# Experts that scale their rows and scatter-add them into one DRAM row per token; a last stage that reads one row and is spread over three engines

## The reference, cut to what matters

```python
x = _layernorm(x + attention(x))
probs = softmax(flat @ gate_W)                       # 4096 tokens x 8 experts
topk_w, topk_idx = top_k(probs, 2); topk_w = topk_w / topk_w.sum(-1)
combine = (one_hot(topk_idx, 8) * topk_w[..., None]).sum(axis=1)
out = 0.5 * gelu(flat @ shared_W + shared_b)
for e in range(8):
    h = gelu(flat @ W1[e] + b1[e])                   # 256 -> 1024
    out = out + combine[:, e:e + 1] * (h @ W2[e] + b2[e])
out = (out - mean) * rsqrt(var + 1e-5) * gamma + beta
x = _layernorm(x + out)
```

## Time and profile before

| | us |
|---|---|
| median of 3 runs | 2104.87 (2103.75 to 2106.13) |
| the profiled execution | 2106.24, of it 2104.6 in the span |
| mean granted TensorE clock | 0.945 |
| DVE busy over the span | 1370.2 |
| PE busy over the span | 1835.4 |
| POOL busy over the span | 212.1 |

### The profile page before, as it was taken

The page is one execution under the profiler, slowest core; times in us unless marked ns, Lnnn a source line. Parts: engine busy times, 40 slices in busy tenths (PEclk is TensorE's granted clock), DMA queues, the critical chain, the costliest instruction groups (busy, mean ns, idle before and its releaser), DMA issues. The chain is left out here.

```text
span 2104.6 us, 31804 instructions
## 1 busy us (share of the span) xinstructions
PE 1835.4 (87%) x10807; PEld 1169.0 (56%) x10808; DVE 1370.2 (65%) x1767; ACT 935.0 (44%) x1362; POOL 212.1 (10%) x295
## 2 busy tenths in 40 slices
PE   2999999999999999999999996998439999999600
PEld 1544454444444445444444442877239999999600
DVE  3577677777767777776776775333766555555388
ACT  3555544455444555445554552122225555555220
POOL 0000000000000000000000000000054444444200
PEclk9999999999999999999999997999669999999855
DMA  7000000000000000000000003442022222222241
GB/s 254 11 21 26 16 21 26 17 20 26 21 16 26 21 16 26 21 21 21 21 26 16 21 16 134 144 156 70 21 79 85 85 85 82 85 82 85 63 154 60
DMA packets 63836, 115.21 MB, mean 55 GB/s; under 512 B 5120, under 2 KB 36224, under 8 KB 61440
## 3 DMA queue, kind: packets, MB, share of 16 engines
q1 hardware_dynamic: 55744, 90.88, 12.7%
q0 software_dynamic: 8000, 23.08, 3.5%
HBM read 79.60 MB, written 34.34 MB: 54 GB/s over the span
## 5 line engine op out<-in xcount | busy, mean ns | idle before, releaser
L418 ACT ACTIVATE a_e<-banks 128x1024 f32<-128x1024 f32 x512 | 496.2, 1022 | 213.4 <-PE banks L334 213.2
L478 DVE TENSOR_TENSOR a_esum<-a_esum,a_e 128x1024 f32<-128x1024 f32 x384 | 469.5, 1223 | 57.5 <-ACT a_e L418 36.3
L348 PE MATMUL banks<-a_e,a_v 128*64 128x512 f32 x2048 | 495.7, 605 | 0.0
L348 PEld LDWEIGHTS banks<-a_e,a_v 128*64 128x64 f32 x2048 | 124.1, 136 | 238.9 <-issue 176.2
L334 PE MATMUL banks<-a_qh,a_kh 64*128 64x512 f32 x1024 | 229.4, 445 | 2.0 <-DVE a_ql L466 1.6
L482 DVE RECIPROCAL a_inv<-banks 128x512 f32<-128x512 f32 x64 | 214.9, 3358 | 15.9 <-PE banks L357 15.9
L475 DVE TENSOR_TENSOR a_esum<-a_e 128x1024 f32<-128x1024 f32 x64 | 78.4, 1225 | 201.9 <-ACT a_e L418 201.9
L334 PE MATMUL banks<-a_ql,a_kh 64*128 64x512 f32 x1024 | 201.5, 390 | 0.0
L334 PE MATMUL banks<-a_qh,a_kl 64*128 64x512 f32 x1024 | 200.8, 389 | 0.0
L1357 ACT ACTIVATE e_g<-banks,e_b1c 128x256 f32<-128x256 f32 x280 | 113.9, 469 | 139.1 <-PE banks L1297 137.8
L334 PEld LDWEIGHTS banks<-a_qh,a_kh 64*128 64x128 f32 x1024 | 95.7, 183 | 139.6 <-issue 123.5
(11 more groups left out here) (206 smaller groups left out, 2733.1 us busy)
## 6 DMA issues: line engine op xcount, KB each, us to landing
attn_out<-a_ot SPq DMA_DIRECT2D x64, 256.0 KB, 2.0
t_ot<-attn_out SPq DMA_DIRECT2D x8, 2048.0 KB, 8.2
a_w<-w_qkv SPq DMA_DIRECT2D x32, 256.0 KB, 3.1
e_w<-w_up SPq DMA_DIRECT2D x8, 1024.0 KB
e_w<-w_down SPq DMA_DIRECT2D x8, 1024.0 KB
o_y<-expert_rows SPq DMA_DIRECT2D x8, 1024.0 KB, 7.8
b_xr<-x_rows SPq DMA_DIRECT2D x4, 1024.0 KB, 12.7
raw<-x_t SPq DMA_DIRECT2D x8, 512.0 KB, 10.5
```

The lines of the kernel that those rows point to most:

```text
L348: mm = pe.matmul(o_acc[slot % 2][h * DH:(h + 1) * DH, :], v[quad % 2][:, n, head], e[n % NE][:, h * BANK:(h + 1) * BANK], start=n == 0, st ...
L418: act.activation(e[n % NE], ring[n % 2], ACT.Exp, scale=SCALE).then_inc(e_ok, 1)
L478: dve.tensor_tensor(acc[:, :], acc[:, :], e[n % NE], ALU.add).then_inc(add_ok, 1)
```

## The change

**Routing.** The two weights, times 2, go into one tile `w_all`, with two more columns of zeros for padding slots. PE turns it, ACT copies it out of PSUM, and SP stores it as `w_rows` in DRAM (66 x 128). SP also copies `shared` (4 MB) to the new DRAM tensor `acc_rows`, one row per token. `places` holds for each slot two numbers: where its weight is in `w_rows`, and which row of `acc_rows` it goes to.

**Experts.** In each chunk POOL gathers the weights of the 256 slots (two more indirect transfers with 4 bytes for each partition) and scatters with an addition in the transfer. ACT scales the bias by the weight; DVE scales the result and adds the scaled bias in one instruction. Since weights are doubled, the sum is twice the reference's before the first layernorm of `outputs`, whose epsilon is four times as large.

**Outputs.** 8 groups of 4 tiles; the rows are read once; ACT normalizes, POOL multiplies by `gamma`, DVE makes the statistics and adds `x2`.

```diff
 def routing(...):
+        @block.sync
+        def _(sp):
+            rows = acc_rows[0:T, :].rearrange("(t p) d -> p t d", p=P)
+            for b in range(B):
+                sp.dma_start(rows[:, b * ST:(b + 1) * ST, :], shared[:, b * ST:(b + 1) * ST, :]).then_inc(shared_out, 16)
+            sp.wait_ge(w_t_ok, 1)
+            sp.dma_start(w_rows, w_t[:, :]).then_inc(w_out, 16)
+            sp.wait_ge(w_out, 16)
+            sp.wait_ge(shared_out, 16 * B)
         @block.gpsimd
+            make_identity(gp, ident, ident_ok)
         @block.tensor                                   # behind the two counting matmuls
+            pe.transpose(banks[3][0:TOPK * TT + CT, 0:P], w_all[:, :], ident[:, :]).then_inc(w_turned, 1)
         @block.scalar                                   # behind the Exp
+            act.wait_ge(w_turned, 1)
+            act.copy(w_t[:, :], banks[3][0:TOPK * TT + CT, 0:P]).then_inc(w_t_ok, 1)
         @block.vector
+            dve.memset(w_all[:, TOPK * TT:], 0.0)
+            dve.tensor_scalar(spare2[:, :, :], spare[:, :, :], float(TOPK * T - T), None, ALU.add)
...
-            link(dve.tensor_tensor(w2[:, :], e2[:, :], w1[:, :], ALU.mult))
+            dve.tensor_scalar(both[:, :, 0:1], w1[:, :].unsqueeze(2), 2.0, None, ALU.mult).then_inc(w_all_ok, 1)
+            dve.scalar_tensor_tensor(both[:, :, 1:2], e2[:, :].unsqueeze(2), 2.0, w1[:, :].unsqueeze(2), ALU.mult, ALU.mult)\
+               .then_inc(w_all_ok, 1)
...
-            link(dve.tensor_tensor(target_f[:, :], target_f[:, :], pad[:, :], ALU.add))
-            link(dve.tensor_copy(target[:, :], target_f[:, :]))
+            for n, (number, beyond) in enumerate(((target_f, spare2), (source_f, spare))):
+                link(dve.tensor_tensor(pad2[:, :], pad[:, :], beyond[:, :, :].rearrange("p a b -> p (a b)"), ALU.mult))
+                link(dve.tensor_tensor(places[:, :, n, :], number[:, :]..., pad2[:, :]..., ALU.add))

 def experts(...):
         @block.gpsimd
-            prime(gp, y_stored)
+            prime(gp, y_stored, y_stored)
...
                         gather(u)
-                        gp.wait_ge(y_ok, c * CT + CT + 1)
-                        numbers(target_c, target, c, target_ok, c + 1)
+                        numbers(places_c[:, :, :].rearrange("p a b -> p (a b)"),
+                                places[:, bass.ds(c, 1), :, :].rearrange("p o a b -> p (o a b)"), places_ok, c + 1)
                         for a in range(CT):
                             gp.indirect_dma_start(
-                                out=expert_rows, in_=y[u][:, a, :], in_offset=None,
-                                out_offset=bass.IndirectOffsetOnAxis(ap=target_c[:, a:a + 1], axis=0)).then_inc(y_out, 16)
+                                out=wt[:, a:a + 1], out_offset=None, in_=w_flat,
+                                in_offset=bass.IndirectOffsetOnAxis(ap=places_c[:, 0, a:a + 1], axis=0)).then_inc(wt_in, 16)
+                        gp.wait_ge(y_ok, c * CT + CT + 1)
+                        gp.nop().then_inc(numbers_ok, 1)
+                        for a in range(CT):
+                            gp.indirect_dma_start(
+                                out=acc_rows, in_=y[u][:, a, :], in_offset=None,
+                                out_offset=bass.IndirectOffsetOnAxis(ap=places_c[:, 1, a:a + 1], axis=0),
+                                compute_op=ALU.add).then_inc(y_out, 16)
                         gp.wait_ge(y_out, c * (16 * CT) + 16 * CT)
         @block.scalar
             act.wait_ge(ident_ok, 2)
+            act.wait_ge(bias_in, 32)
...                                                     # at the end of the chunk's list
+                        act.wait_ge(wt_in, c * (16 * CT) + 16 * CT)
+                        act.wait_ge(y_ok, c * CT + 1)
+                        for a in range(CT):
+                            act.activation(b2w[:, a, :], b2all[:, bass.ds(expert, 1), :].rearrange("p a b -> p (a b)"),
+                                           ACT.Identity, scale=wt[:, a:a + 1]).then_inc(b2w_ok, 1)
         @block.vector
                         dve.wait_ge(y_stored, c + 1)
+                        dve.wait_ge(b2w_ok, c * CT + CT)
                         dve.wait_ge(y_done, c * CT + CT + 1)
                         for a in range(CT):
-                            dve.tensor_tensor(y[u][:, a, :], y_ps[u][:, a * D:(a + 1) * D],
-                                              b2all[...], ALU.add).then_inc(y_ok, 1)
+                            dve.scalar_tensor_tensor(y[u][:, a, :], y_ps[u][:, a * D:(a + 1) * D], wt[:, a:a + 1],
+                                                     b2w[:, a, :], ALU.mult, ALU.add).then_inc(y_ok, 1)

 def outputs(...):                                      # the new lists, GROUP = 4, GROUPS = 8
+            for k in range(GROUPS):                     # SP; gamma is loaded behind group 0
+                sp.dma_start(y[:, tiles(k), :], rows[:, tiles(k), :]).then_inc(rows_in[k], 16)
+            for k in range(GROUPS):
+                sp.wait_ge(norm_ok[1], (k + 1) * GROUP)
+                sp.dma_start(to[:, tiles(k), :], y[:, tiles(k), :]).then_inc(out_sem, 16)
+            for k in range(GROUPS):                     # POOL
+                gp.wait_ge(norm_ok[0], (k + 1) * GROUP)
+                gp.tensor_tensor(y[:, tiles(k), :], y[:, tiles(k), :], g[:, :]..., ALU.mult).then_inc(scaled, 1)
+            deviation(0, 0)                             # ACT: deviation = one Sqrt with epsilon as bias,
+            normalize(0, 0)                             # normalize = 4 Identity with scale and bias
+            for k in range(GROUPS):
+                if k + 1 < GROUPS: deviation(0, k + 1)
+                if k: normalize(1, k - 1)
+                if k + 1 < GROUPS: normalize(0, k + 1)
+                deviation(1, k)
+            normalize(1, GROUPS - 1)
+            statistics(0, 0)                            # DVE: statistics = 4 bn_stats, 4 bn_aggr
+            inverse(0, 0)                               # inverse = one reciprocal, one product with -mean
+            for k in range(GROUPS):
+                if k + 1 < GROUPS: statistics(0, k + 1)
+                if k: inverse(1, k - 1)
+                mix(k)                                  # waits for POOL, adds x2 to 4 tiles
+                if k + 1 < GROUPS: inverse(0, k + 1)
+                statistics(1, k)
+            inverse(1, GROUPS - 1)
```

More of the change, by code:

```diff
@@ L1479, in deviation @@
             def deviation(n, k):
[L1480 to L1491 removed]
+                act.wait_ge(mv_ok[n], k + 1)
@@ new lines, in deviation, with normalize @@
+                act.activation(std[n][:, tiles(k), :], mv[n][:, tiles(k), 1:2], ACT.Sqrt, bias=eps[:, n:n + 1])\
+                   .then_inc(std_ok[n], 1)
+            def normalize(n, k):
+                act.wait_ge(back_ok[n], k + 1)
+                for t in range(k * GROUP, (k + 1) * GROUP):
+                    act.activation(y[:, t, :], y[:, t, :], ACT.Identity, bias=back[n][:, t, :], scale=rstd[n][:, t, :])\
+                       .then_inc(norm_ok[n], 1)
+            act.wait_ge(eps_ok, 2)
@@ L1493, in _ @@
+            deviation(0, 0)
+            normalize(0, 0)
+            for k in range(GROUPS):
+                if k + 1 < GROUPS:
+                    deviation(0, k + 1)
+                if k:
+                    normalize(1, k - 1)
+                if k + 1 < GROUPS:
+                    normalize(0, k + 1)
+                deviation(1, k)
+            normalize(1, GROUPS - 1)
         @block.vector
         def _(dve):
-            steps = [0]
-            def stage(instructions):
-                for ins in instructions:
-                    last = ins
-                steps[0] += 1
-                last.then_inc(chain, 1)
-                dve.wait_ge(chain, steps[0])
@@ L1505, in statistics @@
-            def statistics(n, k):
-                stage(dve.bn_stats(stats[n][:, i, :], y1[:, t, :]) for i, t in enumerate(tiles(k)))
-                stage(dve.bn_aggr(mv[n][:, i, :], stats[n][:, i, :]) for i in range(GROUP))
-                dve.tensor_scalar(var[n][:, :], mv[n][:, :, 1], EPS, None, ALU.add).then_inc(var_ok[n], 1)
-            def normalize(n, k):
-                dve.wait_ge(std_ok[n], k + 1)
-                stage([dve.reciprocal(rstd[n][:, :], std[n][:, :])])
-                for i, t in enumerate(tiles(k)):
-                    ins = dve.tensor_scalar(y1[:, t, :], y1[:, t, :], mv[n][:, i, 0:1], rstd[n][:, i:i + 1],
-                                            ALU.subtract, ALU.mult)
-                return ins
@@ new lines, in statistics @@
+            def statistics(n, k):
+                if n == 0:
+                    dve.wait_ge(rows_in[k], 16)
+                else:
+                    dve.wait_ge(mixed, k + 1)
+                for t in range(k * GROUP, (k + 1) * GROUP):
+                    ins = dve.bn_stats(stats[n][:, t, :], y[:, t, :])
+                ins.then_inc(stats_ok[n], 1)
```

(4 more changed lines are left out.)

150 lines of the change are left out of this document (70 added, 80 removed).

## The result

The changed kernel takes 2291.62 us (2289.45 to 2293.8), against 2105.03 of the kernel before: 1.0887 times as long, 95% interval 1.0868 to 1.0905. Forecast were 2227 us and a range of 2160 to 2310: the direction and the mechanism hold, the size came out half as large again (+187 instead of +122). The time lies inside the range, but nearer to the 2330 of rival D than to the forecast.

A forecast was written before the change was run, and what follows sets the result against it. POOL's serial list was to set the expert loop's pitch, 15.9 us against 11.9. Profiled 2104.6 + 171 for the experts - 50 for the last stage + 1 for routing = 2227 us; range 2160 to 2310.

The forecast's parts named there:

- rival D: Expert loop: scattering with an addition costs 3 us a chunk more than forecast, in POOL's issue or landing; 2330 us; chance 0.09.
- What bounds: Expert loop: POOL's serial list, 9.3 us without its wait, has 2.6 us to spare; the change makes it 15.9.
- Rival E: Expert loop: weights' gather, ACT's scaling and landing hide behind PE, pitch stays 11.9; 2056 us; decides at 13.3; chance 0.05.
- Rival B: Expert loop: idling TensorE falls to its lower clock, for a third of the loop, pitch 19; 2330 us; chance 0.08.
- Rival C: Last stage: POOL's product and DVE shut each other out, +18 us, 2245 us; chance 0.08.
- The signs named beforehand: Loop: POOL's wait for y at least about 3 us, turns 15 to 17, PE gaps; last stage near 61 us.
- the signs against: Pitch near 12, TensorE clock below 0.7, scatter landing waits of 5 us, or four bn_stats rows beyond 2 us.
- the price of the addition: POOL's scatters in the expert loop: 0.5 us a chunk in the transfer, from 0 to 2.0; issuing unchanged at 2.41.
- the changes of expert: Expert loop, where weights load: 7 changes x (3.6 + 1.5) = 35 us, from 10 to 60.
- The last stage: Outputs: 5.9 us a group, 47 for eight; sum 61 against 111 us, a gain of 50, between 30 and 55.
- POOL's lateness: Last stage: POOL's product is late by little behind DVE's statistics and inverse; 0.3 us added to each group.
- Smaller edits: Ahead of the loop: ACT's wait for biases is hidden; routing +1 us; the copy of shared hides in empty DMA.

## Why the prediction was right or wrong

**What bounds, and the direction: right.** POOL's series sets the pitch. It is shown by taking the wait for the weights out of the turn (-116 us), by a third of the matmuls that make no difference (-4), and by adding only the gathers to the kernel before (+70). Rival E needed a pitch under 13.3; measured is 18.50. Rival B: the granted clock in the loop is 0.86, not under 0.7, and the kernel with fewer matmuls shows that it sets nothing. The low clock itself did come, as B feared: after 10.3 us without a matmul (to 1881.54) it is 0.50 from 1882 to 1885, 0.80 in the next 3 us and then 1.00. The turn leaves PE room for it. Rival C: DVE's rows of statistics, without and with POOL's product beside them, and that product:

```profile
2237.12 1.40 DVE L1559 BATCH_NORM_STATS2 o_stats<-o_y 128x6 f32<-128x256 f32 x4
2238.85 1.37 DVE L1559 BATCH_NORM_STATS2 o_stats<-o_y 128x6 f32<-128x256 f32 x4
2240.26 0.38 DVE L1563 BATCH_NORM_AGGREGATE o_mv<-o_stats 128x2 f32<-128x6 f32 x4
```

```profile
2239.40 2.34 POOL L1522 TENSOR_TENSOR o_y<-o_y,o_g 128x1024 f32<-128x1024 f32 x1 [3.74 <-ACT o_y L1535]
```

The product lies beside the last 0.8 of the 1.37 us and beside all of the bn_aggr, which takes 0.38 us with POOL idle too. The Trainium skill says this of instructions with one input ("SBUF — State Buffer", "Who interferes with whom"); the trace agrees. The same rule's other half, an instruction with two inputs, is what 1.45 instead of 0.16 us above shows.

**The signs named beforehand.** As said: POOL's wait for `y` (4.24 us), ACT's wait for the weights' transfer, and PE's gap ahead of each down projection (164.6 us in 34). Not as said: turns of 15 to 17 us (the median is 18.0), a last stage near 61 us and DVE over 8 tenths in it (50.2 busy of 66.8). The lower ends of the working's terms sum to 14.2 and the upper ones to 19.2, where 14.0 and 19.3 stand; nothing hangs on it, and the measured 17.87 lies between. Of the signs against, rival D's landing of 5 us in ordinary chunks did not show (3.54): half of what the addition costs lies in POOL's issue.

**The step that failed: the price of the addition.** The working gave it one term, 0.5 us in the transfer (0 to 2.0), and took the scatters' issuing as before, 2.41. The series from 1882.85 to 1900.72, term by term, forecast in brackets: copy of the sources and row gathers 3.37 (3.30); `places` and the weights' gathers 3.23 (3.30); landing until ACT begins 1.51 (1.4); ACT 0.91 (0.9) and 0.13 more until DVE; DVE 0.88 (0.8); `y` to the first scatter 0.81 (0.6); two scatters 3.49 (2.41); landing and turn 3.54 (2.7 and 0.5). That is 17.87 against 15.9. Against the kernel with plain scatters, where they issue in 1.00 and 1.12 and the next turn begins 2.59 later, the addition costs 1.1 in issuing and 0.95 in landing: 2.0 us where 0.5 stood; the other terms together are 0.5 longer. Rival D named both places and priced them at 3 us more than the forecast's 0.5; it holds in kind, with half its size (1.5 more). 34 x 1.97 = 67 us too little in the series, less 14 too much for the changes of expert (next point), are the 53 by which the loop missed. The kernel with plain scatters is only 51 us faster and not 34 x 2.0 = 68, since its turns ahead of a change are longer. For setup and completion of one transfer the Trainium skill ("DMA: Bandwidth & Descriptors", "Anatomy of one DMA — SWDGE (gpsimd) path") gives a fixed 2.0 us. The trace has 1.51 us from the second gather's issue end to ACT's start, and 2.47 from its issue start; for the term as the working counts it, the row decides.

**The changes of expert**: mean pitch 18.50 against an ordinary 17.9, so 34 x 0.6, some 20 us, where 35 were forecast; right in kind, too large. The forecast took 3.6 us more for the landing at each change; in five of the seven it is 1.3 more (4.7 to 4.9 us against some 3.5), in two 3.3 and 3.6. In sum the loop is +224 instead of +171. Its end was forecast at under 1 us and is +5.7: 1.0 more until the last scatter is issued (2204.09 to 2209.30, before 1980.04 to 1984.25), and 4.7 more from there to the last stage's first load, though the data moved in the first 3 us of it. That stretch is 9.3 us in the kernel before. It does not come with the addition alone: it is 15.2 us with plain scatters, and 15.2 in the kernel before with only the gathers added, against 11.5 there with only the addition and 11.4 with no weight gather. So most of it comes with the gathers in POOL's list; by what, no run shows.

**The last stage**: 66.8 instead of 61 us, so -44.3 instead of -50. The group takes 6.5 instead of 5.9 us, 0.6 x 8 = 5 of the 6. The largest single error is the small instruction that POOL shuts out (1.3 us); the 0.3 that I had added for POOL's lateness was not needed there, and the other terms together are 0.4 smaller than forecast. The two kernels on that instruction show that nothing is won back by freeing it, nor by giving the product to DVE.

**Smaller edits**: ACT's wait for the biases is hidden as said (first `y` at 1575.10, before 1575.01); routing is 2 us longer where 1 was forecast.

**Left open.** Why an adding scatter issues 0.6 us longer. How much of the step from weights gathered ahead to the landing waited for later, and of that from the kernel before to the one with added gathers, is POOL's list, and how much PE's waits for late rows that follow from it: the medians give the list (12.4 and 13.0), the difference of mean and median was taken apart in no run.

## What to carry to other kernels

Before work is added to an engine that issues transfers, add up its list for one turn, with its waits for landings, and compare the sum with the pitch (the time from one turn to the next): here 179 busy of 433 us meant only 2.6 us of 11.9 to spare. Fetch what a turn needs a turn ahead, wait for a landing behind the next thing to issue, and if a small per-row number can ride along in data that is moved anyway, drop its transfer: the same change with the weights carried through the sort and the landing waited for one chunk later is 1.8% faster than the kernel before instead of 8.9% slower. Price an indirect transfer twice, by its issuing on the engine and by its landing; the bytes said little of either here.

## What the runs showed of the hardware

- An indirect scatter of 128 rows of 1 KB takes POOL 0.98 to 1.16 us to issue (65 of 70 in the kernel before) and with an addition 1.57 to 1.67 (55 of 70 in the changed kernel) or 1.81 to 1.83 (the other 15). From the issue's end to the next turn's first row pass 2.56 to 2.90 us where no weights are loaded, with an addition 3.3 to 3.7.
- In the changed kernel a gather of 128 rows of 4 bytes takes POOL as long to issue (0.95 to 0.99 us, 68 of 70) as one of 1 KB (0.95 to 1.06).
- After 4.7 us without a matmul the granted clock was 0.53 in the next 3 us, and 1.00 again 9 us later (weights gathered ahead); after 10.3 us without one it was 0.50, and 1.00 again 6 us later (the changed kernel).
- A DVE instruction with two inputs from SBUF waits for the rest of POOL's product even if it has 4 elements a partition (0.16 becomes 1.0 to 2.0 us); one with one input, bn_stats, doesn't (1.37 against 1.40 us).
